# Three-layer decoder block on one core: tokens packed by token-id expert first, and the first two layers, the second norm and the weight splits in one merged pipeline

## The chip, the cores and the metric

The kernel runs on one core of a Trainium2 chip. The metric is the device time of one execution in microseconds, the median of several runs. The core has five engines with an instruction queue each: PE (TensorE, matmuls and transposes), DVE (VectorE), ACT (ScalarE), POOL (GpSimd) and SP (SyncE, which here only issues DMAs). They wait for one another through semaphores; each engine works its own queue in order.

## The reference

2048 tokens of width 512 pass three residual layers. Cut to what matters:

```python
x = x + attn_ref(layernorm(x), w_gate, g_gate, w_down, g_down)   # layer A: gated MLP, ternary weights, 8-bit activations
x = x + xattn_ref(layernorm(x), token_ids, ctx, ctx, ctx)        # layer B: one of 4 experts, chosen by the token's id
x = x + ffn_ref(layernorm(x), gate_w, w_gate, w_up, ...)         # layer C: shared expert and the best 2 of 8 experts

def attn_ref(x, ...):            # A; bitlinear = rmsnorm, rounding to 255 steps per row, weights rounded to -1, 0, 1
    gate, v = split(bitlinear(x, w_gate, g_gate))                # 512 -> 2 * 1408
    return bitlinear(gate * sigmoid(gate) * v, w_down, g_down)   # 1408 -> 512

def xattn_ref(h, token_ids, W, W, W):   # B
    e = min(clip(token_ids, 0, 24999) // 6250, 3)
    return ((silu(h @ W[e].T) * (h @ W[e].T)) @ W[e].T)          # the same 512 x 512 matrix three times

def ffn_ref(h, ...):             # C
    p = softmax(h @ gate_w.T); top 2 of 8
    return sum over the top 2 of p_e * expert_e(h) + shared(h)   # experts 512 -> 352 -> 512, shared 512 -> 704 -> 512
```

## The kernel before

Tokens are worked in tiles of 128 rows, 16 of them (T). Products of B and C are made from 16-bit high and low parts, three matmuls for each (`split_product`: high by high, high by low, low by high). Every layer is a software pipeline: `pipeline(engine, count, stages)` takes a list of (lag, stage) and, in round r, runs each stage on tile r minus its lag, in the order of the list. So the order within a list is the order of an engine's queue within a round, and the lag is how many rounds a stage runs behind. In the middle of a list it makes a hardware loop of two rounds (`Fori`).

- **Routing for B.** At the start DVE and PE compute, from the token ids, where each token goes when tokens are sorted by expert, with each expert padded to whole tiles: 19 tiles (J_B). `invB` lists the tokens of each padded tile, `posB` the place of each token.
- **Layer A** (16 tiles plus fill and drain). SP loads x in token order. DVE: statistics, `swiglu` in four chunks per tile, `g_absmax`, `norm1` (L1052), `d_int` (L1026) and others. POOL: the gains product in two halves (L597), small vectors, `h_lo` (L621). ACT: silu, roundings, evacuations of PSUM. PE: `gate_up` in four chunks of 8 matmuls of 352 columns (L1299), `d_turn` with 11 transposes (L1307), `down` with 11 matmuls of 512 columns (L1316), `x_turn` with 4 transposes. The result x1 is stored, and its norm as high and low halves in `hB_d`. The context matrix is loaded and split during the last rounds (`ctx_chunks`).
- **Layer B** (19 tiles). It starts when all of `hB_d` is stored. POOL gathers the rows of a padded tile, PE transposes them (8 transposes, L1330), ACT evacuates them (L795), then `b_first` (12 matmuls), silu and product, four transposes (L1360), `b_second` (12 matmuls), and a store to `yB_d`. 18 of the 40 chunks of C's expert weights (`wstage`, 544 KB each) are loaded and split beside it, one a round (`split_hi` L789 on ACT, `split_lo` L1102 on DVE).
- **Second norm, stage S** (16 tiles). It starts when all of `yB_d` is stored, and runs in the first 15 rounds of C (S_ROUNDS). SP loads x1, POOL gathers y rows (L630), `residual2` (L1124), statistics, `norm2`, `s_rest`, stores of x2 and `hC_d`, a transpose and the router product (`s_turn`, `s_router`).
- **Layer C.** Rounds 0 to 23 (R0 = 24) work 12 tiles of the shared expert, two halves each; the other 22 weight chunks are split beside them, and after S the top-2 routing is computed on DVE in eight pieces with one C round after each (`beside`). Rounds 24 to 62 are 39 routed tiles (gather, products, store to `yC_d`). The last 8 rounds work the remaining 4 shared tiles, while POOL gathers the two expert rows of every token (L687), DVE sums them (L1246) and SP stores the output in pairs of tiles (`f_store`).

SP's queue has in every round of S, in this order: the next weight chunk (`s_loadw`), `s_stored` (which waits until the stores of x2 and hC of an earlier tile have landed), loads for C, the store of x2, the store of hC, and the load of x1.

## Time and profile before

| | us |
|---|---|
| median of 3 runs | 937.57 (936.64 to 939.38) |
| profiled execution, first to last instruction | 967.5 |
| PE busy | 760.4 (79%) |
| DVE busy | 504.4 (52%) |
| ACT busy | 397.7 (41%) |
| POOL busy | 263.6 (27%) |
| moved by DMA | 127.57 MB, mean 132 GB/s |
| mean granted TensorE clock | 0.912 |

The profiled execution is 29.9 us longer than the median. Its record has a start and a length for each instruction; the times of this document are read on that scale, from the first instruction. PE's busy time is that of matmuls which overlap, so a PE that is 100% busy at full clock sets the pace, and one at 70% may still wait in every round.

### The profile page before, as it was taken

The numbers are of one execution on the slowest core, as the hardware profiler recorded it, in microseconds if no ns is written. First come the engines' busy times: TensorE is split into PE (matmuls) and PEld (weight loads), VectorE is DVE, ScalarE is ACT, GpSimd is POOL, SyncE is SP. The second block draws the span as 40 slices with busy tenths as digits, with TensorE's granted clock in tenths as the row PEclk, the third lists the DMA queues.
The fourth block names the chain that finished last, engine by engine and source line by source line (L and its number), as shares of the span: only waits on it lengthen the run. The fifth ranks groups of instructions, "written<-read, shape, count | busy, mean of one in ns | idle before, by whom it ended". The sixth has DMA issues, their size and how long they took to land.

```text
span 967.5 us, 17562 instructions
## 1 busy us (share of the span) xinstructions
PE 760.4 (79%) x5001; PEld 452.5 (47%) x5017; DVE 504.4 (52%) x861; ACT 397.7 (41%) x567; POOL 263.6 (27%) x401
## 2 busy tenths in 40 slices
PE   0457777777429999749778998899999999999275
PEld 0234443444215555335445655566666666665133
DVE  6779888887714555446564567222222222222146
ACT  5866556656515555335343543122332223231010
POOL 1235665565321111032121000111111111104710
PEclk9979899888559999969898999899999999999679
DMA  9312222212544555267776542122222222226843
GB/s 353 112 34 77 61 70 87 87 66 87 158 159 135 180 179 179 95 209 238 230 215 216 201 148 78 56 88 87 76 77 86 87 78 77 84 77 224 248 138 138
DMA packets 51204, 127.57 MB, mean 132 GB/s; under 512 B 6496, under 2 KB 6496, under 8 KB 50528
## 3 DMA queue, kind: packets, MB, share of 16 engines
q1 hardware_dynamic: 42688, 99.33, 30.5%
q0 software_dynamic: 8480, 27.79, 9.9%
q8 instruction: 19, 0.31, 0.1%
q14 instruction: 17, 0.14, 0.1%
HBM read 87.78 MB, written 39.32 MB: 131 GB/s over the span
## 4 chain that ended last, share of the span: by engine, by line
PE 47%; DMA 10%; issue 4%; another core or an unknown queue 4%; DVE 4%; SPq 2%; ACT 1%; POOL 0%; DVEq 0%; POOLq 0%; ACTq 0%
PE banks L1338 41%; DMA x_d<-w_hi 5%; PE banks L1330 3%; PE banks L1428 2%; DMA x_d<-yrow 2%; DMA hC_d<-w_lo 1%; PE banks L1360 1%; DMA rows<-hC_d 1%; DVE w_hi L1246 0%; DMA rows<-hC_d,idx 0%; SPq L458 0%; SPq L441 0%; DVE w_lo L1102 0%; DMA rows<-hB_d,idx 0%
## 5 line engine op out<-in xcount | busy, mean ns | idle before, releaser
L1338 PE MATMUL banks<-w_hi,hT 128*128 (+1 forms) x1288 | 321.0, 326 | 4.4 <-issue 3.2
L1338 PE MATMUL banks<-w_lo,hT 128*128 (+1 forms) x644 | 209.8, 326 | 0.0
L1338 PEld LDWEIGHTS banks<-w_hi,hT 128*128 128x128 f16 x1288 | 128.0, 99 | 82.2 <-issue 10.6
L1338 PE MATMUL banks<-w_hi,cpT 128*128 (+1 forms) x426 | 142.9, 390 | 10.0 <-issue 8.6
L1299 PE MATMUL banks<-w_hi,w_lo 128*128 128x352 bf16 x384 | 89.3, 350 | 45.6 <-DVE w_hi L1015 34.3
L844 ACT ACTIVATE cs<-banks 128x352 f32<-128x352 f32 x71 | 32.9, 463 | 201.7 <-PE banks L1338 175.5
L1160 DVE TENSOR_TENSOR cs<-banks,cs 128x352 f32<-128x352 f32 x71 | 37.1, 523 | 140.9 <-ACT cs L844 135.0
L1164 DVE TENSOR_TENSOR cpT<-banks,cpT 128x384 f16<-128x384 f32 x71 | 39.5, 556 | 129.3 <-ACT cpT L849 112.6
L1338 PE MATMUL banks<-w_lo,cpT 128*128 (+1 forms) x213 | 83.1, 390 | 5.3 <-issue 5.3
L1330 PE MATMUL banks<-eyeH,rows 128*128 128x128 f16 x584 | 47.6, 225 | 48.2 <-DMA rows<-hC_d 19.6
L1338 PEld LDWEIGHTS banks<-w_lo,hT 128*128 128x128 f16 x644 | 63.9, 99 | 34.5 <-issue 0.8
L849 ACT CAST cpT<-banks 128x384 f16<-128x384 f32 x71 | 33.9, 478 | 96.3 <-PE banks L1428 80.5
L1299 PEld LDWEIGHTS banks<-w_hi,w_lo 128*128 128x128 bf16 x384 | 38.0, 107 | 73.1 <-DVE w_hi L1015 41.5
L628 POOL COPY idx<-invC 128x1 int32 (+1 forms) x39 | 7.1, 182 | 235.6 <-PE banks L1330 163.5
L1338 PEld LDWEIGHTS banks<-w_hi,cpT 128*128 128x128 f16 x426 | 42.3, 99 | 58.7 <-issue 18.6
L1330 PEld LDWEIGHTS banks<-eyeH,rows 128*128 128x128 f16 x584 | 40.0, 101 | 60.6 <-issue 32.5
L839 ACT COPY hT<-banks 128x1024 f16<-128x1024 f16 x55 | 55.6, 1012 | 24.9 <-PE banks L1330 24.9
L597 POOL TENSOR_TENSOR w_hi<-w_hi 128x704 f32<-128x704 f32 x32 | 54.2, 1694 | 32.6 <-DVE w_hi L1015 32.3
L1102 DVE SCALAR_TENSOR_TENSOR w_lo<-wstage,w_hi 128x1088 f32 (+1 forms) x40 | 51.4, 1285 | 4.8 <-ACT w_hi L789 4.8
L1338 PE MATMUL banks<-w_hi 128*128 x152 | 48.3, 379 | 2.3 <-DVE yrow L1116 2.3
L1316 PE MATMUL banks<-w_lo 128*128 128x512 bf16 x161 | 43.9, 427 | 5.0 <-ACT w_lo L751 3.8
L630 POOL DMA_INDIRECT rows<-hC_d,idx x39 | 38.0, 974 | 33.6 <-POOL idx L628 32.4
...
## 6 DMA issues: line engine op xcount, KB each, us to landing
...
yC_d<-yrow SPq DMA_DIRECT2D x39, 256.0 KB, 2.0
w_hi<-x_d SPq DMA_DIRECT2D x20, 256.0 KB
yB_d<-yrow SPq DMA_DIRECT2D x19, 256.0 KB, 2.0
w_hi<-in_wgate SPq DMA_DIRECT2D x3, 1408.0 KB, 9.9
w_hi<-in_x SPq DMA_DIRECT2D x16, 256.0 KB, 2.8
w_lo<-in_x SPq DMA_DIRECT2D x16, 256.0 KB, 3.6
x_d<-w_lo SPq DMA_DIRECT2D x16, 256.0 KB, 2.9
```

The costliest lines, as they stand in the source:

```text
L597: pool.tensor_tensor(swg[s.u][:, at], sw[s.u][:, at], gd[:, at], ALU.mult).then_inc(swg_done, 1)
L630: pool.indirect_dma_start(out=dst[s.u][:] if dst is rows else dst[s.u], out_offset=None, in_=table[:, :], in_offset=bass.IndirectOffsetOnA ...
L839: act.copy(hT[s.u][:].rearrange("p a n -> p (a n)"), bank(0).bitcast(F16)).then_inc(c_ev, 1)
L844: act.activation(cs[:, 0:IC], bank(1 + s.u, IC), ACT.Silu, scale=1.0 / SCALE_C).then_inc(c_sil, 1)
L849: act.copy(cpT[:, 0, :], bank(5, ICP)).then_inc(c_hi_s, 1)
L1102: dve.scalar_tensor_tensor(out=w_lo[:, at], in0=wstage[s.u][:], scalar=SCALE_C, in1=w_hi[:, at], op0=ALU.mult, op1=ALU.subtract).then_inc( ...
L1160: dve.tensor_tensor(cs[:, 0:IC], bank(3 + s.u, IC), cs[:, 0:IC], ALU.mult).then_inc(c_p, 1)
L1164: dve.tensor_tensor(cpT[:, 1, :], bank(5, ICP), cpT[:, 0, :], ALU.subtract).then_inc(c_lo_s, 1)
L1299: mm = pe.matmul(bank(2 * half + c % 2, CW), xqT[s.u][:, k * P:(k + 1) * P], wgT[k][:, at:at + CW], start=(k == 0), stop=(k == KD - 1))
L1316: mm = pe.matmul(bank(7), qdT[s.u][:, k * P:(k + 1) * P], wdT[:, k * D:(k + 1) * D], start=(k == 0), stop=(k == KI - 1))
L1330: mm = pe.transpose(bank(0).bitcast(F16)[:, k * P:(k + 1) * P], source[:, k * P:(k + 1) * P], eyeH[:])
L1338: mm = pe.matmul(to, a(k, pa), w(k, pw), start=(begins and k == 0 and n == 0), stop=(ends and k == steps - 1 and n == 2))
```

## The change

Where each token goes is still computed first, but without padding: `packing` gives `invT`, the tokens in order of their expert, 16 full tiles. From there on all stages work in packed order:

- POOL gathers the rows of x for A twice with that list (`gather_x` for the statistics, `gather_res` for the residual); SP's `load_x` and `load_res` go.
- A tile of B is a window of 128 consecutive packed rows at a computed row `baseB` (`padded_tiles`); it may reach into a neighbour's rows, which are then written again by the tile that owns them. So `b_gather`, the 8 PE transposes and ACT's evacuation go; one DMA that transposes while it moves (`b_load`, `DMA_TRANSPOSE`) brings the window from `hB_d` into `hT`. It and the store `b_store` read their row from `baseB` into a register of SP first.
- B tile j needs only the A tiles up to j, so B runs in the same rounds as A, `b_first` 5 rounds behind (B_LAG) and `b_second` 6. S runs in the same list too: its first tile in round 16. C's round 0 is round 25 (C0). All lists of these 25 rounds are written out straight, without a hardware loop.
- S needs no gather: y is in order. Its POOL gathers go; SP loads y (L512). Its stages are spread wider: `s_stored` is two rounds behind the store it waits for.
- The context matrix is loaded and split in rounds 1 to 4. Weight chunks: 8 in rounds 17 to 24, then two in each of C rounds 0 to 8, then one each.
- Several stages change places in their lists; `b_rows_out` goes from DVE to ACT. PSUM banks are dealt out anew.
- S ends in C round 9 (S_ROUNDS = 10), and the routing pieces stand beside C rounds 10 to 17.
- The output goes out in packed order, so it is scattered row by row: 16 indirect DMAs on POOL, behind its 32 gathers, each waiting for the sum of its tile.

```diff
+B_LAG = 5
+C0 = T + 3 + B_LAG + 1
+S_LAG = T - C0
-S_ROUNDS = T - 1
+S_ROUNDS = T + S_LAG + 3
...
-        CTX_FROM = T + 3 - CTX_ROUNDS
+        CTX_FROM = 1
...
+        W_ONES, W_TWOS = 8, 9
+        W_FROM = C0 - W_ONES
...
+            def b_load(s):
+                if s.t == 0:
+                    sp.wait_ge(routeB, 2)
+                for u in range(2):
+                    sp.wait_ge(hb_out[u], 16 * ((covered(s.t + 1) + 1 - u) // 2))
...
+                before(sp, b_t, s.t, 2)
+                sp.sem_inc(passed["sp"], 1)
+                at = sp.value_load(baseB[0:1, s.t:s.t + 1], min_val=0, max_val=N)
+                sp.dma_start_transpose(hT[s.u][:], hB_d[bass.ds(at, P), :]).then_inc(b_hT[s.u], 16)
...
-            pipeline(sp, TILES, [(W_LAG - 1, s_loadw, w_rest), (-2, s_stored, whole), (-2, c_rows_in, shared_first),
-                                 (-3, s_storex2, whole), (-3, s_storeh, whole), (-5, s_load, whole), (1, c_store),
-                                 (0, c_sum_in, shared_first)], end=S_ROUNDS)
...
+            twos, ones = w_twos(load_w), w_ones(load_w)
+            w_loads = [(twos[0] - 1, *twos[1:]), (ones[0] - 1, *ones[1:])]
+            s_stages = shifted([(2, s_stored), (0, s_storex2), (1, s_storeh), (-1, s_load)], -S_LAG)
...
-            pipeline(pool, T, [(-2, small_x), (1, small_g), (3, small_b), (0, lambda s: gains(s, 0)),
-                               (0, lambda s: gains(s, 1)), (3, h_lo)])
...
+            def gather_x(s):
+                if s.t == 0:
+                    pool.wait_ge(routeB, 1)
...
+                pool.indirect_dma_start(out=xin[s.u], **packed(x, s)).then_inc(x_in[s.u], 16)
...
+            straight(-4, C0, [(-4, gather_x), (-2, small_x), (3, small_b), (1, small_g), (0, lambda s: gains(s, 0)),
+                              (2, gather_res), (3, h_lo), (0, lambda s: gains(s, 1)), (T, s_rstd)])
...
+            for n in range(T):
+                alone(pool, "pool", f_o, n + 1)
+                pool.indirect_dma_start(out=out[:, :], out_offset=bass.IndirectOffsetOnAxis(ap=invT[:, n:n + 1], axis=0),
+                                        in_=xF[:, n * D:(n + 1) * D], in_offset=None).then_inc(f_out, 16)
...
+            stages = [(3, residual1), (B_LAG + 1, b_rest, all_b), (0, lambda s: swiglu(s, 0)), (3, spread1), (3, moments1),
+                      (1, g_absmax), (B_LAG, b_prod, all_b), (0, lambda s: swiglu(s, 1)), (-3, x_spread), (-3, x_moments),
+                      (1, g_reciprocal), (1, g_factor), (-2, x_reciprocal), (-2, x_factor), (3, norm1), (-1, x_int),
+                      (-3, x_center), (1, d_int), (0, lambda s: swiglu(s, 2)), (-3, x_absmax), ctx_chunks(ctx_rest),
+                      (0, lambda s: swiglu(s, 3))]
...
-            pe.wait_ge(ctx_lo, CTX_CHUNKS)
-            pe.wait_ge(x1_done, T)
-            pipeline(pe, J_B, [(0, b_first), (-1, b_turn), (1, b_second), (0, b_turn_a)])
...
+            stages = [(0, lambda s: gate_up(s, 0)), (B_LAG, b_first, all_b), (0, lambda s: gate_up(s, 1)), (2, d_turn),
+                      (B_LAG + 1, b_second, all_b), (0, lambda s: gate_up(s, 2)), (-1, x_turn), (2, down),
+                      (0, lambda s: gate_up(s, 3)), (B_LAG, b_turn_a, all_b)]
```

PE, a round of layer A. Before, between two chunks of `gate_up` (L1299) stand only the transposes of `d_turn` (L1307) and `down` (L1316):

```order
L1299 MATMUL banks<-w_lo 128x352
L1307 MATMUL banks<-w_lo 128x128 [waits d_ev,d_q]
L1307 MATMUL banks<-w_lo 128x128 x10
L1299 MATMUL banks<-w_hi,w_lo 128x352 [waits sw_done]
L1299 MATMUL banks<-w_hi,w_lo 128x352 x2
L1299 MATMUL banks<-w_lo 128x352
L1299 MATMUL banks<-w_hi,w_lo 128x352 x3
L1299 MATMUL banks<-w_lo 128x352
L1316 MATMUL banks<-w_lo 128x512 [waits x1_done,d_ev]
L1316 MATMUL banks<-w_lo 128x512 x10
```

PE, the same place now, from round 6 on (L1423 is `gate_up`, L1433 `d_turn`, L1490 the load of the expert's number, L1458 B's products):

```order
L1423 MATMUL banks<-w_lo 128x352
L1433 MATMUL banks<-w_hi,w_lo 128x128 [waits d_ev,b_lo,x_ev,d_q]
L1433 MATMUL banks<-w_hi,w_lo 128x128 x10
L1490 TENSOR_LOAD expB [waits b_lo,x1_done]
L1490 ISA x2
L1458 ISA
L1458 MATMUL banks<-w_hi,w_lo 128x512
L1458 REGISTER_ALU
L1458 MATMUL banks<-w_lo 128x512
```

What moved: `b_second`'s 12 matmuls stand between `d_turn` and the third chunk, and in the same way `b_first`'s 12 between the first and the second.

DVE, the end of a round of layer A and the start of the next. Before (`norm1` L1052, `d_int` L1026, `residual1` L1034, `swiglu` L1015, `g_absmax` L1021):

```order
L1052 TENSOR_SCALAR w_lo<-w_lo,mv,rstd 128x512 [waits lo_done,hi_done,rs1]
L1002 TENSOR_SCALAR cg<-cg,smG 128x1 [waits g_rec]
L978 SCALAR_TENSOR_TENSOR w_hi<-w_hi,xmv 128x512 [waits x_mom,x_mag]
L1010 REGISTER_ALU
L1015 SCALAR_TENSOR_TENSOR w_hi<-banks,dqx,w_hi 128x352 [waits sil_done]
L983 TENSOR_REDUCE xmax<-w_hi 128x1 [waits x_cen]
L1026 TENSOR_SCALAR w_lo<-w_hi 128x1408 [waits d_T,d_mag]
```

DVE now (`norm1` L1186, `x_int` L1141, `d_int` L1160, `swiglu` L1149):

```order
L1186 TENSOR_SCALAR w_lo<-w_lo,mv,rstd 128x512 [waits lo_done,hi_done,rs1]
L1141 TENSOR_SCALAR w_lo<-w_hi 128x512 [waits x_T,x_mag]
L1112 SCALAR_TENSOR_TENSOR w_hi<-w_hi,xmv,w_lo 128x512 [waits x_mom,x_q]
L1160 TENSOR_SCALAR w_lo<-w_hi 128x1408 [waits d_T,d_mag]
L1149 SCALAR_TENSOR_TENSOR w_hi<-banks,dqx,w_hi 128x352 [waits sil_done]
L1117 TENSOR_REDUCE xmax<-w_hi 128x1 [waits x_cen]
L1149 SCALAR_TENSOR_TENSOR w_hi<-banks,dqx,w_hi 128x352 [waits sil_done]
```

What moved: `d_int` stood behind the last `swiglu` of a round, whose end also starts POOL's second half of the gains; now it stands before the last two.

SP, one round of C with S beside it, inside the loop. Before (L441 weight chunk, L484 rows for C, L462 x2, L467 hC, L458 load of x1):

```order
L441 DMA wstage<-in_wmoe 128x1088
L484 ISA [waits s_hout0,s_x2out0,c_T]
L484 DMA rows<-hC_d 128x1024
L462 ISA [waits s_x2]
L462 DMA x_d<-w_hi 128x512
L467 ISA [waits s_lo,s_hi]
L467 DMA hC_d<-w_lo 128x1024
L458 ISA [waits s_h,s_x2out1]
L458 DMA w_hi<-x_d 128x512
```

SP now, in C rounds 0 to 8 (L500 weight chunk, L516 x2, L521 hC, L510 load of x1, L512 load of y, L547 rows for C):

```order
L500 DMA wstage<-in_wmoe 128x1088 [waits wlo_done] x2
L516 DMA x_d<-w_hi 128x512 [waits s_hout1,s_x2out1,s_x2]
L521 DMA hC_d<-w_lo 128x1024 [waits s_lo,s_hi]
L510 DMA w_hi<-x_d 128x512 [waits x1_out0,b_out1,s_h,s_x2out0]
L512 DMA w_lo<-yB_d 128x512 [waits s_x2]
L547 DMA rows<-hC_d 128x1024 [waits c_T]
```

What moved: two weight chunks are ahead of the loads of x1 and y; the second waits for the round's last `split_lo` on DVE.

## Rows read from the trace of the kernel before

**Rows 1.** Stretches: length, PE, PEld, DVE, ACT, POOL busy, clock, DMA, GB/s

```profile
57.00:267.00 210.00, 149.23 (x856) 83.11 (x869) 178.01 (x278) 126.34 (x197) 118.72 (x159) 0.84 0.27 85
285.00:404.00 119.00, 115.54 (x664) 61.36 (x664) 58.30 (x74) 56.99 (x74) 19.05 (x33) 0.97 0.47 150
541.00:612.00 71.00, 66.16 (x486) 41.14 (x484) 45.39 (x97) 28.06 (x39) 0.18 (x1) 0.98 0.36 120
```

**Rows 2.** Timeline of a round of layer A: start, us, engine, instruction [idle before]

```profile
140.95 2.18 DVE L1026 TENSOR_SCALAR w_lo<-w_hi 128x1408 bf16<-128x1408 f32 x1
149.94 0.61 PE L1299 MATMUL banks<-w_hi,w_lo 128*128 128x352 bf16 x3
150.54 0.61 PE L1299 MATMUL banks<-w_hi,w_lo 128*128 128x352 bf16 x3
154.06 1.67 POOL L597 TENSOR_TENSOR w_hi<-w_hi 128x704 f32<-128x704 f32 x1 [1.83 <-DVE w_hi L1015]
154.30 2.18 DVE L1026 TENSOR_SCALAR w_lo<-w_hi 128x1408 bf16<-128x1408 f32 x1
```

**Rows 3.** Two lines of DVE alone: min/median/max ns, first and last start

```profile
L1026 DVE TENSOR_SCALAR w_lo<-w_hi x16: 889/2180/2186, 64.4 to 258.2; 128x1408 bf16<-128x1408 f32 x16
L1052 DVE TENSOR_SCALAR w_lo<-w_lo,mv,rstd x16: 546/1882/1893, 84.4 to 270.0; 128x512 f32<-128x512 f32 x16
```

**Rows 4.** Chain of work in a round of layer B: start, us, what

```profile
296.35 0.45 PE banks L1330 x8
296.79 2.59 PE banks L1338 x12
299.38 0.44 PE banks L1360 x4
299.82 2.59 PE banks L1338 x12
```

**Rows 5.** Timeline of the start, DVE and PE

```profile
15.85 0.18 DVE L939 CAST invB<-banks 128x19 int32<-128x19 f32 x1 [0.53 <-PE banks L1268]
20.64 0.69 DVE L983 TENSOR_REDUCE xmax<-w_hi 128x1 f32<-128x512 f32 x1
23.77 0.16 DVE L1073 TENSOR_REDUCE wmean<-banks 128x1 f32<-128x4 f32 x1 [0.33 <-PE banks L1278]
37.43 1.06 PE L1299 MATMUL banks<-w_hi,w_lo 128*128 128x352 bf16 x3 [11.31 <-DVE w_lo L1083]
56.52 1.06 PE L1299 MATMUL banks<-w_hi,w_lo 128*128 128x352 bf16 x3 [8.15 <-DVE w_hi L1015]
```

**Rows 6.** DMA issues by line: KB each, median us from issue to landing

```profile
w_hi<-in_wgate SPq DMA_DIRECT2D x3, 1408.0 KB, 9.9
hB_d<-rows SPq DMA_DIRECT2D x16, 256.0 KB, 2.1
rows<-hC_d SPq DMA_DIRECT2D x15, 256.0 KB, 4.0
rows<-hB_d,idx POOLq DMA_INDIRECT x19, 3.8
```

**Rows 7.** SP's waits in stage S: us in total, times, longest; then residual2

```profile
SPq L458 <- DMA x_d<-w_hi: 38.0, 11, 4.6
L1124 DVE SCALAR_TENSOR_TENSOR w_hi<-w_lo,w_hi x16: 684/684/693, 414.7 to 535.7; 128x512 f32<-128x512 f32 x16
```

**Rows 8.** One issue on SP (timeline), then the page's group of weight splits on DVE

```profile
479.01 0.36 SPq L462 DMA_DIRECT2D x_d<-w_hi  x1
...
L1102 DVE SCALAR_TENSOR_TENSOR w_lo<-wstage,w_hi 128x1088 f32 (+1 forms) x40 | 51.4, 1285 | 4.8 <-ACT w_hi L789 4.8
```

**Rows 9.** Chain of two shared rounds of layer C, late in the program

```profile
872.23 5.52 PE banks L1338 x33
884.04 0.34 PE banks L1428 x3
```

**Rows 10.** The page's DMA queue of SP: packets, MB, share of 16 engines

```profile
q1 hardware_dynamic: 42688, 99.33, 30.5%
```

606 lines of the change are left out of this document (350 added, 256 removed).

## The prediction

> **What bounds the kernel now.** Read the stretches first, then look inside each for the wait that ends last. The kernel has four regimes. In layer A, 57 to 267 us, DVE is busy 178.01 of 210 us and PE's clock is granted at 0.84 only [rows 1]: a round takes 13.35 us, the distance of two `d_int` [rows 2], and DVE sets it. Part of that is not work. `d_int` has a median of 2.18 us and once took 0.89; `norm1` has 1.88 and 0.55 at best [rows 3]. In the timeline `d_int` starts 0.24 us behind a POOL product of 1.67 us and ends some 0.75 us behind its end [rows 2]: the two share something, and DVE loses 1.3 us twice, 2.6 us a round. In layer B, 285 to 404 us, PE is the bound: 115.54 of 119 us busy at clock 0.97 [rows 1], and the chain is PE alone, 0.45 + 2.59 + 0.44 + 2.59 = 6.07 us a tile [rows 4]. In stage S the 16 `residual2` are (535.7 - 414.7)/15 = 8.07 us apart, and SP stood 38.0 us waiting for stores of x2 before it issued the next load [rows 7]: a loop through memory sets the pace. From 541 to 612 us nine shared rounds take 71 us [rows 1], though two such rounds need 884.38 - 872.23 = 12.15 us of PE [rows 9], 6.08 each: 16 us go to the routing computed between them. The 39 routed tiles after 612 us and the last shared ones are not changed.
>
> So until 612 us PE works well in B only. The change lays B, which needs PE, beside A, which needs DVE, and hides the emptying of A, the start of B and the start of S. The sum goes by the time at which the first routed round starts, 612 us before.
>
> **Start.** x is gathered only after the packing is known. The last small step of the old routing ends at 16.03 us, and two tiles' statistics were done at 21.33 [rows 5], 5.3 us later; the weights' mean followed at 23.77. The packing has about as many small steps. A gather lands 3.8 us after issue when the queues are quiet; a weight load in this stretch took 9.9 [rows 6]. Statistics then end at 25 to 31 us instead of 21.3, the mean 1.5 to 7 us late. I take 4, nearer to the gather's own row: the first `gate_up` at 41.4 instead of 37.4. Round 0 keeps its length, 56.52 - 37.43 = 19.1 [rows 5], so round 1 starts at 60.5.
>
> **Rounds 1 to 4** have no B yet but all eight context splits. DVE loses the 2.6 us of contention if the new order holds (`d_int` no longer behind the end of the last `swiglu`) and gains two splits of about 1.29 [rows 8]: still 13.3 a round, 53, to 113.7.
>
> **Rounds 5 to 15, A and B together.** PE at full clock: 32 matmuls of `gate_up` at 0.60 us per four (149.94 to 150.54) [rows 2], 4.8; 11 of `down` at 2.59/12 each, 2.4; 15 transposes at 0.45/8, 0.85; B 2 x 2.59 + 0.44, 5.6 [rows 4]. Sum 13.65 us. B's own turn, 0.45, is gone. DVE: 178.01/210 x 13.35 = 11.3, less 2.6, plus two 128x512 steps of 0.68 [rows 7], 10.1, or 12.7 if the contention stays. ACT: 126.34/210 x 13.35 = 8.0 plus three such steps, 10.0 [rows 1]. PE becomes the bound, its idle DVE and ACT hide their additions. Bounds: 13.65, and 16.3 if the contention's 2.6 us stay and stop PE too. I take 14.7: the register load ahead of each B product was hidden under 2.6 us of queued matmuls before, and now has one chunk of 1.2 us ahead. 11 x 14.7 = 162, to 275.4.
>
> The Trainium skill, VectorE: DVE Perf Modes, section "The three transpose paths", gives 1309 ns for a 128x128 transposed by DMA; eight one after another would be 10.5 us a tile, an estimate from that page, and 19 us would be added below by its price. No trace here shows a DMA that transposes.
>
> **Rounds 16 to 24, the rest of B beside S.** Rounds 16 to 18 still have `d_turn`, `down`: PE 5.6 + 3.0 + 0.45 for S's turn, about 9.1; I take 10, 30 us. Then S's loop: a load lands 4.0 us after issue [rows 6], `residual2` 0.7, statistics 0.9, the halves 0.7, three issues of 0.36 [rows 8], 7.4; PE needs about 7. I take the measured 8.1 of S before. Six rounds are 48.6, to 354.0. The transposing DMA is issued a round ahead, so up to about 8 us are hidden here and 14 before. Its cost is in no row. Below: the plain store of the same 256 KB lands in 2.1 us. Near: the gather of the same rows lands in 3.8 [rows 6]. Above: a packet took 0.305 x 16 x 967.5/42688 = 0.11 engine-us [rows 10]; cut into pieces of 256 B the tile is 1024 packets, 7.1 us on 16 engines; in pieces of 128 B, 14.2. I take anything below 8, which costs nothing.
>
> **C rounds 0 to 9.** Here the change adds a wait. SP may issue the second weight chunk only after the last split of DVE's round, and x2, hC, the loads of x1 and y are queued behind it, and `residual2` of the next round behind those. Five issues of 0.36 [rows 8], 1.8; landing 4.0 [rows 6]; then on DVE 0.7 + 0.9 + 0.7, about 1.0 for C's steps, two splits 2.6 [rows 8]. Sum 11.7 us a round, six times, 70; the last S tiles are done by round 6. Round 0 about 9, rounds 7 and 8 with two chunks 8 each, round 9 8. Sum 103, to 457. Bounds for the six: 8.1, the pace of S before with one chunk, and 14.
>
> **C rounds 10 to 23.** 14 x 6.08 = 85 [rows 9], and of the 16 us of routing I keep 14, since its end is no longer the start of the gathers: 99. The first routed round starts at 556, that is 56 us earlier.
>
> **End.** The last store was plain and is now an indirect DMA behind the sum: between 0 and 3.8 us [rows 6], 1.5 taken. The other scatters hide under the last shared rounds.
>
> Sum: 967.5 - 56 + 1.5 = 913 us for a profiled execution. That of before is 29.9 us longer than the median. I put the difference, not a ratio, on the median: 937.57 - 54.5 = **883 us**.
>
> **Rivals.**
>
> - *The doubled weight chunks cost nothing.* If the loads of x1 and y land sooner than DVE's other work ends, S stays at 8.1: 6 x 3.6 = 22 us less, and with a merged round of 14.0 another 8: 853 to 861. For it: SP's waits for stores, 38.0 us, are gone by the wider lag. Against: 1.1 MB more stand ahead of those loads.
> - *The contention stays, or the transposing DMA is a little too slow.* Merged rounds of 16.3: 11 x 1.6 = 18 us more, 901. POOL has two more issues a round, so this is open. Or a transposed tile of 10 to 12 us: only the eight tiles of rounds 16 to 23 feel it, 8 x (11 - 8.1) = 23 us, 906.
> - *Slower than before.* The place is the load of `hT` in B. With T us a tile, T above 8.1 costs 8 (T - 8.1), and above 14.7 also 11 (T - 14.7); the 54.5 us are gone at T = 14.9. Pieces of 128 B give 14.2, almost that; at 20 us a tile 95 + 58 = 153 us are lost and the kernel takes 1036. Stores of A's results and the weight chunks share SP's queue, so it would hit them as well.
> - *Nothing moves*, because the other engines' queues bind at the same places: against it stands that DVE, ACT and PE all have room for the sum of both layers in a 13.35 us round, as worked out.
>
> **How the numbers follow.** The forecast with 868 to 898 has 0.45. The first rival, down to 845, 0.17; still faster 0.02. The second, 898 to 925, 0.22; more of it, to 934, 0.05. Within 0.3%, which is about what a measurement of this kernel tells from no change, 0.02. Slower 0.07. Faster is 0.91. The range 848 to 922 leaves out some 0.18: the slower case, the upper part of the second rival and a little below.
>
> **What would show it.** Layer A's rounds from 5 on 14 to 15.5 us long, PE over 90% busy at a clock near 1; `d_int` and `norm1` near 0.9 and 0.6 us; the first `gate_up` at 39 to 44 us; `hT` landing in under 8 us, and no wait of `b_first` for it; C rounds 1 to 6 about 12 us apart with DVE waiting for the load of y; the first routed round at about 556 us. Wrong would be made most easily by the transposing DMA, then by waits between the four engines inside a merged round, which add up where each queue is in order.

## The result, and the profile after

The changed kernel takes **966.26 us** (median of 4 runs, 965.62 to 969.98), the kernel before beside it 937.11 (4 runs, 934.96 to 939.38). The ratio is 1.031, 95% interval 1.028 to 1.034: **slower by 3.1%**, where 883 us were forecast. 83 us have to be accounted for.

Busy time by stretch of the changed kernel, cut where the forecast cuts (columns as in [rows 1]): rounds 1 to 4, 5 to 15, 16 to 24, C rounds 0 to 9, C rounds 10 to 23, and from the last matmul to the end.

```profile
68.43:127.20 58.77, 37.07 (x183) 19.19 (x187) 45.17 (x74) 35.24 (x52) 28.80 (x40) 0.73 0.32 99
127.20:287.80 160.60, 150.08 (x921) 85.02 (x931) 117.99 (x214) 106.25 (x170) 99.96 (x134) 0.98 0.34 101
287.80:390.10 102.30, 71.45 (x424) 36.28 (x425) 54.88 (x92) 42.45 (x60) 20.37 (x33) 0.90 0.69 207
390.10:539.40 149.30, 80.51 (x579) 49.26 (x580) 53.82 (x88) 44.65 (x59) 6.44 (x14) 0.72 0.45 147
539.40:636.00 96.60, 90.05 (x611) 55.13 (x610) 57.41 (x111) 42.29 (x56) 2.70 (x6) 0.98 0.38 128
938.00:968.30 30.30, 0.24 (x2) 0.00 (x0) 5.82 (x9) 0.00 (x0) 17.23 (x17) 0.58 0.42 156
```

| | forecast, us | measured, us | difference |
|---|---|---|---|
| first `gate_up` at | 41.4 | 49.1 | +7.7 |
| round 0 | 19.1 | 19.4 | +0.3 |
| rounds 1 to 4 | 53 | 58.8 | +6 |
| rounds 5 to 15 (A and B together) | 162 | 160.6 | -1 |
| rounds 16 to 24 | 78.6 | 102.3 | +24 |
| C rounds 0 to 9 | 103 | 149.3 | +46 |
| C rounds 10 to 23 | 99 | 96.6 | -2 |
| first routed round at | 556 | 636 | +80 |
| last sum to the end | about 5 | 24.3 | +19 |

The forecast has no figure for the last row; it is the 3.3 us of the kernel before without its stall (below) and the 1.5 that the forecast adds.

The merged rounds came out at the forecast length: PE is busy 150.08 of 160.6 us at clock 0.98, against 0.84 for layer A alone in [rows 1]. The largest loss is in C rounds 0 to 9: PE is busy 54% of the time there, at a granted clock of 0.72, with DMA at 0.45 and DVE at 36%. No engine is full there; they wait for one another. The waits of that stretch (waiter <- what it waited for: us in total, times, longest):

```profile
PE banks L1450 <- DMA rows<-hC_d: 68.3, 5, 18.0
DVE w_hi L1211 <- DMA w_lo<-yB_d: 45.8, 6, 8.0
```

L1450 are the transposes of the shared expert's rows (`c_turn`), L1211 is `residual2`. One round on SP's queue, DVE and PE, from the timeline (start, us, engine, line; in brackets the idle time before and its releaser):

```profile
399.39 2.48 DVE L1197 SCALAR_TENSOR_TENSOR w_lo<-wstage,w_hi 128x1088 f16<-128x1088 f32 x2
400.70 1.53 SPq L500 DMA_DIRECT2D wstage<-in_wmoe  x2
402.42 0.35 SPq L516 DMA_DIRECT2D x_d<-w_hi  x1
402.87 0.37 SPq L521 DMA_DIRECT2D hC_d<-w_lo  x1
403.42 0.34 SPq L510 DMA_DIRECT2D w_hi<-x_d  x1
403.81 1.41 SPq L512 DMA_DIRECT2D w_lo<-yB_d  x1
405.26 0.75 SPq L547 DMA_DIRECT2D rows<-hC_d  x1
410.73 0.69 DVE L1211 SCALAR_TENSOR_TENSOR w_hi<-w_lo,w_hi 128x512 f32<-128x512 f32 x1 [7.96 <-DMA w_lo<-yB_d]
411.41 1.01 PE L1450 MATMUL banks<-eyeH,rows 128*128 128x128 f16 x8 [10.64 <-DMA rows<-hC_d]
421.22 1.53 SPq L500 DMA_DIRECT2D wstage<-in_wmoe  x2
```

Read it from the top. The two splits of the last round (L1197) free the two weight buffers; SP, which stood waiting for exactly that, issues two chunks of 544 KB, then two stores, then the loads of x1 and y, then the shared rows. Those land at 410.7 and 411.4, with the chunks under way beside them. Only then can `residual2` and `c_turn` start, and behind them in DVE's queue stand the next two splits, which end the loop at 421.22: 20.5 us for this round. The next took 14.5 (the chunks' next issue is at 435.68), and so they alternate, up to 523.4. The long ones are those that load shared rows (L547 at 405.26, 440.15, 474.17 and 507.00), since one load of rows serves two halves: there PE's part, and behind it the splits, wait for the rows too.

At the other end, GpSimd issues the 32 gathers of `yC_d` and then the 16 scatters of the output; the last sum of DVE is L1369:

```profile
896.74 0.95 POOL L746 DMA_INDIRECT w_lo<-yC_d,posC  x1 [28.93 <-DMA yC_d<-yrow]
937.77 1.27 POOL L746 DMA_INDIRECT w_hi<-yC_d,posC  x1 [0.30 <-DVE w_hi L1369]
939.35 1.01 POOL L752 DMA_INDIRECT out_x<-w_hi,invT  x1 [0.30 <-DVE w_hi L1369]
943.21 0.75 DVE L1369 SCALAR_TENSOR_TENSOR w_hi<-w_hi,wtop 128x512 f32<-128x512 f32 x1
959.13 0.97 POOL L752 DMA_INDIRECT out_x<-w_hi,invT  x1 [0.30 <-issue]
```

The first scatter goes out at 939.35, when all sums but three are done, and the other fifteen at 1.3 us each. No engine but GpSimd works from 944 us on. Its last issue ends at 960.1 and lands 2.7 us after it began; from 963 us to the end at 968.3 no engine works and no DMA moves anything.

### The profile page after: what moved, and what is told of

Read it like the earlier page. It is cut to its first block, busy times and chain, and to the rows that moved or that the text cites. A ratio compares the mean times of both kernels' runs of the same rounds, so it can differ in the third digit from the quotient of the medians.

```text
span 968.3 us, 16660 instructions
## 1 busy us (share of the span) xinstructions
PE 741.1 (77%) x4848; PEld 441.0 (46%) x4865; DVE 471.0 (49%) x848; ACT 396.4 (41%) x570; POOL 272.6 (28%) x380
## 3 DMA queue, kind: packets, MB, share of 16 engines
q0 software_dynamic: 9520, 31.20, 10.4%
## 4 chain that ended last, share of the span: by engine, by line
PE 55%; DVE 12%; issue 11%; DMA 7%; POOL 6%; ACT 4%; SPq 1%; POOLq 1%; DVEq 0%; ACTq 0%
PE banks L1458 41%; PE banks L1443 4%; PE banks L1423 3%; PE banks L1450 3%; DMA rows<-hC_d 3%; PE banks L1550 2%; DVE w_lo L1197 2%; DMA w_lo<-yB_d 2%; ACT w_hi L847 2%; POOL out_x L752 1%; POOL w_hi L697 1%; DMA w_hi<-in_x,invT 1%; DVE w_lo L1141 1%; DVE w_hi L1149 1%; POOL smA L646 1%
## 5 line engine op out<-in xcount | busy, mean ns | idle before, releaser
L1458 PE MATMUL banks<-w_hi,hT 128*128 (+1 forms) x1288 | 318.2, 324 | 10.9 <-issue 4.5
L1458 PE MATMUL banks<-w_lo,hT 128*128 (+1 forms) x644 | 208.5, 324 | 0.0
L1458 PEld LDWEIGHTS banks<-w_hi,hT 128*128 128x128 f16 x1288 | 127.0, 99 | 88.2 <-issue 17.3
L1458 PE MATMUL banks<-w_hi,cpT 128*128 (+1 forms) x426 | 145.2, 396 | 1.3 <-DVE cpT L1288 1.3
L1423 PE MATMUL banks<-w_hi,w_lo 128*128 128x352 bf16 x384 | 81.5, 326 | 19.1 <-DVE w_lo L1265 10.8
L1450 PE MATMUL banks<-eyeH,rows 128*128 128x128 f16 x440 | 35.6, 227 | 68.3 <-DMA rows<-hC_d 68.3
L1458 PE MATMUL banks<-w_lo,cpT 128*128 (+1 forms) x213 | 84.5, 397 | 0.0
L1458 PEld LDWEIGHTS banks<-w_lo,hT 128*128 128x128 f16 x644 | 63.4, 98 | 34.2 <-issue 0.6
L1458 PE MATMUL banks<-w_hi,w_lo 128*128 x152 | 53.3, 414 | 18.1 <-DVE w_lo L1206 9.7
L1458 PEld LDWEIGHTS banks<-w_hi,cpT 128*128 128x128 f16 x426 | 43.0, 101 | 47.9 <-issue 8.4
L1450 PEld LDWEIGHTS banks<-eyeH,rows 128*128 128x128 f16 x440 | 30.4, 102 | 75.3 <-DMA rows<-hC_d 54.1
L1423 PEld LDWEIGHTS banks<-w_hi,w_lo 128*128 128x128 bf16 x384 | 38.3, 102 | 46.7 <-DVE w_lo L1265 11.0
L632 POOL TENSOR_SCALAR var<-mv 128x1 f32<-128x1 f32 x32 | 9.6, 299 | 174.6 <-DVE mv L1223 121.3
L1197 DVE SCALAR_TENSOR_TENSOR w_lo<-wstage,w_hi 128x1088 f16<-128x1088 f32 (+1 forms) x40 | 50.8, 1287 | 15.6 <-ACT w_hi L847 15.6
L1149 DVE SCALAR_TENSOR_TENSOR w_hi<-banks,dqx,w_hi 128x352 f32<-128x352 f32 x64 | 37.0, 578 | 38.1 <-ACT w_hi L785 38.1
```

The lines of the kernel that those rows point to most:

```text
L1149: dve.scalar_tensor_tensor(out=sw[s.u][:, c * CW:(c + 1) * CW], in0=bank(2 + c % 2, CW), scalar=dqx[s.u][:], in1=sil[c % 2], op0=ALU.mult, ...
L1197: dve.scalar_tensor_tensor(out=w_lo[:, at], in0=wstage[s.u][:], scalar=SCALE_C, in1=w_hi[:, at], op0=ALU.mult, op1=ALU.subtract).then_inc( ...
L1423: mm = pe.matmul(bank(2 * half + c % 2, CW), xqT[s.u][:, k * P:(k + 1) * P], wgT[k][:, at:at + CW], start=(k == 0), stop=(k == KD - 1))
L1450: mm = pe.transpose(bank(0).bitcast(F16)[:, k * P:(k + 1) * P], source[:, k * P:(k + 1) * P], eyeH[:])
L1458: mm = pe.matmul(to, a(k, pa), w(k, pw), start=(begins and k == 0 and n == 0), stop=(ends and k == steps - 1 and n == 2))
```

## A stall in the tail that must be kept apart

The profile of the kernel before, 30 us above its median, has a stall between 889 and 928 us: PE is busy 13.5 of these 39 us, DVE 4.5 and ACT 1.5, with PE and DVE waiting mostly on "issue" and ACT 25.9 us on what the profile calls "remote", while GpSimd issues its gathers back to back. By their times the runs of the result have it in neither kernel. In the batches of experiments, each of which timed the kernel before beside the others, it came and went for all kernels of a batch together, though not in the same length for each; the kernel before took 966.78, 967.55, 937.32, 936.56 and 968.86 us in five batches (7 runs each), the last three on the same chip. So below, totals are compared only within a batch, and stretches by their traces. Two more profiles of the kernel before frame it:

> The kernel before, unchanged, profiled once more. Its first profile has a stretch from 889 to 928 us in which PE, ACT and DVE wait on 'issue' while GpSimd issues its 32 gathers of yC_d, and its span (967.5 us) is 30 us above the median of the runs. If the stall belongs to the profiled execution only or comes and goes, this span is about 937 to 940 us, the last hT copies stand 12 us apart to the end, and the last matmul ends near 928 us. If the stall is in every execution, the span is again 965 to 970 us with the same gap, and then the runs without a profile have it too, in part.

Measured 970.78 us, with the stall: the copies of `hT` (L839) for the last tiles stand 46 and 14 us apart instead of 12, and between 898 and 925 us PE issues single transposes and matmuls 0.7 to 2.8 us apart.

```profile
882.55 1.01 ACT L839 COPY hT<-banks 128x1024 f16<-128x1024 f16 x1
928.68 1.01 ACT L839 COPY hT<-banks 128x1024 f16<-128x1024 f16 x1
942.71 1.01 ACT L839 COPY hT<-banks 128x1024 f16<-128x1024 f16 x1
```

> The kernel before, unchanged, one more profile. Without the stall: the last five hT copies 12.15 us apart each, the last sum 47 us behind the third last copy, the end 4 us behind the last sum, a span of about 935 us. With it: a span of 965 to 970 us again.

Measured 936.63 us. This is the kernel before without the stall:

```profile
622.60 0.46 ACT L844 ACTIVATE cs<-banks 128x352 f32<-128x352 f32 x1 [3.25 <-PE banks L1338]
878.92 1.01 ACT L839 COPY hT<-banks 128x1024 f16<-128x1024 f16 x1
891.06 1.01 ACT L839 COPY hT<-banks 128x1024 f16<-128x1024 f16 x1
907.53 1.01 ACT L839 COPY hT<-banks 128x1024 f16<-128x1024 f16 x1 [4.30 <-PE banks L1330]
930.66 0.75 DVE L1246 SCALAR_TENSOR_TENSOR w_hi<-w_hi,wtop 128x512 f32<-128x512 f32 x1
```

The last gap is still 16.5 us, 4 more than the others. Its first routed silu (L844) is at 622.60, that of the changed kernel at 640.38: **17.8 us are lost before the routed rounds**. From there to the end it takes 934.7 - 622.6 = 312.1 us, the changed kernel 968.3 - 640.4 = 327.9: **15.8 us are lost behind them**: 21.0 from the last sum to the end (24.3 against 3.3), less 5.2 up to the last sum, 4.3 of which are that gap. The first of the two numbers is less firm than it looks: the changed kernel's first routed silu comes at 634.05 in its second profile and at 633.26 to 639.43 in the kernels below that differ from it only in the tail.

## The experiments

**The changed kernel in a batch with the stall.**

> The changed kernel, unchanged, timed in turn with the kernel before on one chip. The kernel before has now shown two tails: without a stall (937 us in the runs shown first) and with one (967 us in seven executions beside the last four kernels, in both profiles: 30 us in which every engine but GpSimd waits on 'issue' while GpSimd issues 32 gathers). The changed kernel's profile had no such stall. If the stall belongs to the chip or the moment of loading, the two kernels fall into it together and the difference stays 25 to 35 us (before 937, changed 966; or 967 and 995 to 1000). If it belongs to each kernel by itself, the changed kernel stays at 966 and the kernel before is at either 937 or 967.

Measured 986.06 us against 967.55, ratio 1.017 (1.011 to 1.023). Its trace has the stall as well (48 us between two `hT` copies that stood 12 apart in the profile after). Both kernels fall into it together, but the difference is 18.5 us, below the 25 to 35 of the first theory. The trace shows what fits that: GpSimd goes on issuing during the stall, its last scatter goes out 1 us behind the last sum, and the end comes 10 us behind that sum, not 24. So the scatters cost some 20 us only where nothing else is late. The stages before the tail agree with the profile after within 6.5 us.

**Where the weight chunks stand on SP's queue.** Two kernels, one that puts the loads first (the same way in rounds 16 to 24), one that puts the chunks last:

```diff
-            s_stages = shifted([(2, s_stored), (0, s_storex2), (1, s_storeh), (-1, s_load)], -S_LAG)
-            c_stages = [(-2, c_rows_in, shared_first), (1, c_store), (0, c_sum_in, shared_first)]
+            early = [*shifted([(-1, s_load)], -S_LAG), (-2, c_rows_in, shared_first)]
+            s_stages = shifted([(2, s_stored), (0, s_storex2), (1, s_storeh)], -S_LAG)
+            c_stages = [(1, c_store), (0, c_sum_in, shared_first)]
...
-            pipeline(sp, TILES, [w_loads[0], *s_stages, *c_stages], begin=2, end=W_TWOS - 1)
+            pipeline(sp, TILES, [*early, w_loads[0], *s_stages, *c_stages], begin=2, end=W_TWOS - 1)
```

> The changed kernel; on the SP queue the loads of x1 and yB (second norm) and of the shared expert's rows stand first in their round, ahead of the weight chunks, whose issue waits for the split of the round before. Theory 1 (order of the SP queue): C rounds 0 to 9, 17.2 us each in the changed kernel, fall to 9 to 12 us, the 8 us that DVE waits for yB in each round and the 11 to 18 us that PE waits for the rows go, and the rounds 17 to 24 lose 2 to 3 us each too: 50 to 80 us less, 890 to 915 us. Theory 2 (traffic: 1.1 MB of weight chunks in each of these rounds, so the loads land late wherever they are issued; or DVE's work): rounds stay at 15 to 17 us, 945 to 966 us.

```diff
-            pipeline(sp, TILES, [w_loads[0], *s_stages, *c_stages], begin=2, end=W_TWOS - 1)
+            pipeline(sp, TILES, [*s_stages, *c_stages, w_loads[0]], begin=2, end=W_TWOS - 1)
```

> The changed kernel; in C rounds 0 to 9 the two weight chunks are issued behind the loads and stores of their round, the rest of the order as it is. Theory 1 (a wait for the split stands ahead of the loads): the loads of yB are issued up to 3 us earlier, but still behind two waits (x2 stored, hC rows stored), so a part of the gain: 10 to 50 us less, 915 to 955 us. Theory 2 (traffic or DVE's work): no change, 960 to 970 us.

Measured 937.58 (4 runs) and 938.25 us (one run), in a batch with the stall, where the kernel before took 966.78 (ratio of the first 0.969, 0.965 to 0.973). The 890 to 915 us forecast for the first were reckoned without the stall; the changed kernel with the stall took 986.06 in the batch above, 48 more. The stretch of C rounds 0 to 9 of the first, and its waits:

```profile
390.46:484.60 94.14, 73.25 (x580) 45.84 (x581) 54.18 (x88) 44.93 (x59) 6.70 (x14) 0.90 0.69 219
...
PE banks L1451 <- DMA rows<-hC_d: 19.3, 4, 7.0
```

149.3 us became 94.1; DMA's share rose from 0.45 to 0.69 and the granted clock from 0.72 to 0.90; DVE's wait for y is out of the longest ones, and the loads of x1 and y land in 2.7 and 3.1 us (medians) where they took 5.1 and 5.3. The same bytes and the same instructions, so traffic and work are not the cause: the **order on SP's queue** is, 55 us (49 to 56 when the way from the first C product to the first routed silu is compared over all profiles with the old order). The second kernel shows that the place of the chunks alone does it: its first routed silu is at 585.96 us, that of the first at 586.31. One part of the theory fell: in rounds 16 to 24 the early loads of the first kernel moved nothing (first C product at 390.46 us, 390.10 in the changed kernel; 391.12 in the second kernel, which leaves those rounds as they are).

**Where `down` stands on PE's queue.**

```diff
-                      (B_LAG + 1, b_second, all_b), (0, lambda s: gate_up(s, 2)), (-1, x_turn), (2, down),
+                      (B_LAG + 1, b_second, all_b), (0, lambda s: gate_up(s, 2)), (2, down), (-1, x_turn),
```

The reason to try it is in round 3 of the changed kernel, DVE's `norm1` (L1186) and `x_int` (L1141), then PE's `x_turn` (L1409) and `down` (L1443):

```profile
103.39 1.24 DVE L1186 TENSOR_SCALAR w_lo<-w_lo,mv,rstd 128x512 f32<-128x512 f32 x1
104.55 0.41 DVE L1141 TENSOR_SCALAR w_lo<-w_hi 128x512 bf16<-128x512 f32 x1
105.02 0.61 PE L1409 MATMUL banks<-w_hi,w_lo 128*128 128x128 bf16 x4 [6.28 <-DVE w_lo L1141]
105.84 4.43 PE L1443 MATMUL banks<-w_lo 128*128 128x512 bf16 x10 [0.22 <-issue]
```

> The changed kernel; on TensorE, down (11 matmuls of the tile two behind) stands ahead of x_turn (4 transposes of the next tile) instead of behind it. In rounds 1 to 4 of the changed kernel (16 to 19 us each, forecast 13.3) TensorE waits 5 to 6.3 us for x_int with down queued behind that wait. Theory: down fills the wait and the four rounds lose 3 to 4 us each; rounds 5 to 15 (14.7 us, TensorE full) stay: d_turn of tile 15 comes 10 to 16 us earlier than 304. Rival: x_int moves with TensorE, since the wait is DVE's and GpSimd's chain (gains, gather, three small chains): no change, 303 to 304 us, or later.

Measured 974.07 us (one run), with the stall, 12 below the changed kernel in the same batch. The last `d_turn` is evacuated at 289.08 instead of 304.16 us (301.1 to 306.4 in all profiles with the old order). Half of that is not where it was expected: the evacuations (L814) of rounds 6 and 7, in the middle of the merged rounds,

```profile
143.88 1.33 ACT L814 COPY w_lo<-banks 128x1408 bf16<-128x1408 bf16 x1
157.48 1.33 ACT L814 COPY w_lo<-banks 128x1408 bf16<-128x1408 bf16 x1
```

stand 13.60 us apart, against 14.71 in the changed kernel (151.81 and 166.52): the six merged rounds that had taken 14.7 lost 1.1 us each. In the changed kernel each of the five of them that lie between 166 and 240 us has PE idle before `x_turn`, and here none has:

```profile
185.90 0.40 PE L1409 MATMUL banks<-w_hi,w_lo 128*128 128x128 bf16 x4 [0.93 <-DVE w_lo L1141]
```

13.6 is the sum of PE's instructions that the prediction gives as the lower bound (13.65). The 1.05 us that it added for a register load ahead of B's products were this wait. Behind 240 us the changed kernel's own rounds take 13.6 to 13.9 already.

**The first gathers.** The 2.8 MB of down weights are issued behind them:

```diff
+            sp.wait_ge(x_in[1], 16)
             sp.dma_start(wd32, wdown[:]).then_inc(wd_in, 16)
```

> The changed kernel; the 2.8 MB load of the down weights is issued once the first two gathers of x have landed, instead of ahead of them. In the changed kernel the first gather, issued at 17.0 us, lands at 26.9 (9.9 us, where later gathers take 3.6). Theory: it shares the DMA engines with the weights (22.7 us for those 2.8 MB), so it now lands in 4 to 6 us and the first gate_up starts 4 to 6 us earlier, at 43 to 45 us. Rival: a gather's first issue is slow by itself, or the four gate loads are what it shares with: it still takes 8 to 10 us and gate_up starts at 48 to 50 us; then the late down weights cost up to 5 us in round 0.

Measured 980.46 us (one run), with the stall. The first tile's statistics, in the changed kernel and here, both behind a gather issued at 17.0 us:

```profile
26.92 0.69 DVE L1100 BATCH_NORM_STATS2 xstats<-w_hi 128x6 f32<-128x512 f32 x1 [8.39 <-DMA w_hi<-in_x,invT]
```
```profile
20.60 0.69 DVE L1101 BATCH_NORM_STATS2 xstats<-w_hi 128x6 f32<-128x512 f32 x1 [2.03 <-DMA w_hi<-in_x,invT]
```

The gather takes 3.6 us instead of 9.9: it had shared the DMA engines with the weights. Only 3.0 us reach the first `gate_up` (45.8 against 48.8 in the same batch), less than the 4 to 6 of the theory: PE waits for the last ternary weights (DVE's L1266) there.

**The output's order.** Scatters between the gathers:

```diff
+            OUT_LAG = 4
...
+                if n >= OUT_LAG:
+                    scatter(n - OUT_LAG)
+            for n in range(T - OUT_LAG, T):
+                scatter(n)
```

> The changed kernel; each output scatter is issued four tiles behind its gathers, between them, instead of all 16 behind all 32 gathers. Theory A (GpSimd's issue, 1.25 us a gather and 1.27 us a scatter, is the bound of the end): 48 issues take 60 us from 897 us, all the same, and the last scatter goes out at about 957 instead of 959 us, since the queue is full in both orders: at most 5 us less, 961 to 966 us. Theory B (the scatters wait for the last sums): the end comes 15 to 20 us earlier, about 947 to 951 us.

Measured 977.85 us (971.9 to 981.68; 1.011 of the kernel before, 1.006 to 1.016), outside both forecasts, in a batch with the stall and without the changed kernel, so the total decides nothing; its last gather leaves at 959.52 us instead of 937.77. In `e9_all` below, without the stall, the end comes 72.4 us behind the first gather, 71.6 in the changed kernel. Interleaving gains nothing: GpSimd's queue is full either way. Then the same output by plain stores, which leaves its rows in packed order (part of the computation left out):

```diff
-                pool.indirect_dma_start(out=out[:, :], out_offset=bass.IndirectOffsetOnAxis(ap=invT[:, n:n + 1], axis=0),
-                                        in_=xF[:, n * D:(n + 1) * D], in_offset=None).then_inc(f_out, 16)
...
+                sp.wait_ge(f_o, n + 1)
+                sp.dma_start(tiles(out, n), xF[:, n * D:(n + 1) * D]).then_inc(f_out, 16)
```

> The changed kernel without the reordering of its output: the 16 output tiles are written by plain stores on the SP queue, in packed order, not by 16 indirect scatters on GpSimd behind its 32 gathers (so the rows of the output stand in another order than the reference's). If GpSimd's in-order issue is the price, the time from the last sum (944 us) to the end falls from 24 us to about 4 to 6 us (four stores at 12 us in the kernel before): some 18 to 20 us less where the rest is as in the changed kernel. If the indirect writes themselves are slow whoever issues them, or the end waits for something else, less than 8 us.

Measured 981.0 us (one run), with the stall: 2.5 us from the last sum to the end, where the changed kernel of the same batch needed 10. The stall covers most of the price, so it was measured once more without it, on top of three of the mended orders:

> Three of the mended orders (loads, down, down weights), and the output by 16 plain stores on SP in packed order (so its rows stand in another order than the reference's). The kernel with four of them, whose scatters run between GpSimd's gathers, ends 72.4 us behind its first gather of yC_d. Theory A (16 more issues of 1.27 us on GpSimd are the price): here the end comes 50 to 53 us behind the first gather, 20 us less, about 875 us on a chip without the stall. If the indirect writes cost no more than plain ones: 68 to 72 us.

Measured 868.73 us (one run), in a batch without the stall (kernel before 936.56). GpSimd's first issue and DVE's last sum:

```profile
815.70 0.95 POOL L751 DMA_INDIRECT w_lo<-yC_d,posC  x1 [28.93 <-DMA yC_d<-yrow]
863.15 0.75 DVE L1372 SCALAR_TENSOR_TENSOR w_hi<-w_hi,wtop 128x512 f32<-128x512 f32 x1
```

The end comes 51.1 us behind the first gather, 21.3 less than with scatters between the gathers and 20.5 less than in the changed kernel. That is the price of putting the output back in token order. In the changed kernel 16 us of it are GpSimd's issues behind the last sum (944.0 to 960.1). The rest is what follows the last issue: 8.2 us there, 2.7 of them or less for the landing, while with plain stores the end comes 2.9 us behind the last sum. Why nothing moves in the last 5 us and more of the kernels with scatters is not shown.

**All four orders, and two tiles in flight.** Loads first (in the C rounds), `down` first, down weights later, scatters between:

> Four orders of the changed kernel mended at once: in C rounds 0 to 9 the loads stand ahead of the weight chunks on the SP queue (54 us earlier at the first routed round, measured); down ahead of x_turn on TensorE (15 us, measured); the down weights' load behind the first gathers (3 us, measured); each output scatter four tiles behind its gathers. If the gains add, the first routed hT copy comes at about 559 us (changed kernel 628 to 634) and the whole takes 966 - 72 - 3 = about 891 us without the stall at the end, 905 to 915 with it; against the kernel before 0.94 to 0.95 in either case. If the faster A and B rounds hand their gain to the drain (rounds 17 to 24, bound by a chain across engines), the first routed copy comes at 565 to 575 us.

Measured **895.65 us** against 937.32, ratio 0.958 (0.952 to 0.963): faster than both kernels. The gains add, near enough: the first routed silu is at 563.68 us, 77 earlier than in the first profile of the changed kernel (70 than in its second) where the three parts measured alone make 72, and the merged rounds keep their 13.6 us.

The gathers of `yC_d` held to two tiles at a time, to see whether queued gathers cause the stall:

```diff
-                if turn > 0:
-                    alone(pool, "pool", f_y[slot], turn * 32)
+                if n >= 2:
+                    alone(pool, "pool", f_y[(n - 2) % 4], ((n - 2) // 4 + 1) * 32)
```

> The changed kernel; GpSimd lets two tiles' gathers of yC_d be under way, not four, before it issues the next. Theory S (the stall at the end is the other engines' instruction loading, which waits behind the queued gathers on the DMA engines): with half as many queued the hT copies of the last four tiles come closer together (48 us between the third last and the second last in the stalled profiles, 12 without a stall), by 15 us or more, and the end comes 10 to 30 us earlier than 986. Rival (the stall comes with the chip or from elsewhere, however many gathers are queued): again 45 to 50 us there and 980 to 990 us, or, on a chip without the stall, 966 to 972 us.

> The four mended orders with two tiles' gathers in flight. By theory S 885 to 900 us, 0 to 25 us below the same kernel with four in flight; by the rival the same as that kernel within 5 us.

> The kernel before with two tiles' gathers in flight instead of four. Where the kernel before takes 967 us (with the stall), theory S says 937 to 955 us; the rival says 965 to 970. Where it takes 937 us there is nothing to see.

Measured 972.77 (one run), 900.84 (ratio 0.961, 0.956 to 0.967) and 952.47 us (one run). The batch had no stall, so the theory about it was not put to the test. What they show is the price: with the kernel before the last gather goes out at 940.83 instead of 919.25 us, and it takes 15 us more; 5 more for the mended kernel. The first has no partner in its batch.

**Rounds 16 to 24.** First theory: SP waits for the result of `b_second` of its own round before it can issue the next transposing load. B's store one round later takes that wait away:

```diff
-            stages = [(3, store_x1), (4, b_load, all_b), (B_LAG + 1, b_store, all_b),
+            stages = [(3, store_x1), (4, b_load, all_b), (B_LAG + 2, b_store, all_b),
```

> The changed kernel; SP stores the result of a layer-B tile one round later (7 rounds behind its gate_up, not 6), so that it no longer waits for the b_second of the round in which it stands, and the next transposing load of hT, the loads of the second norm and the weight chunk behind it are issued earlier. Theory (the drain's round is a loop b_second, copy, SP's wait, SP's issues, transposing load 5.3 us, b_first, b_second): rounds 16 to 24, 102 us from 288 to 390 us in the changed kernel, fall to 80 to 92 us, and TensorE no longer waits for hT there. Rival (DVE's chain of products, norm and split binds, 10 to 11 us a round by itself): they stay at 98 to 104 us.

> The four mended orders and B's store a round later. If the gains add, 10 to 20 us below the same kernel without it (895.65 us on a chip where the kernel before took 937.32): 876 to 886 us on a chip without the stall, ratio to the kernel before 0.935 to 0.945. By the rival no change: 893 to 898 us, 0.955 to 0.96.

Measured 972.92 (one run) and 895.56 us (ratio 0.956, 0.950 to 0.962), without the stall: nothing gained, the first C product is at 392.09 us. The theory is refuted, and the chain of waits in that kernel shows what is there in its place, one round of 9.33 us:

```profile
343.07 0.48 PE banks L1450 x8
...
344.48 1.12 ACT w_hi L847
...
345.69 1.15 issue
346.83 0.54 DVE w_hi L1229
347.37 0.61 DVE w_lo L1206
...
348.92 2.76 PE banks L1458 x12
351.68 0.44 PE banks L1480 x4
352.12 0.28 PE banks L1458 x12
352.40 0.48 PE banks L1450 x8
```

PE's turn of the second norm, ACT's copy of it and the weights' high half (L847), DVE's low half ("issue" at 345.69 is the time of L1197), `norm2`, `b_rest` (L1206), and only then `b_second`. The split of the weights, put at the end of ACT's and DVE's rounds, stands ahead of layer B's `b_split` and `b_rest`. The next pair moves both halves into waits of their engines:

```diff
-            drain = [*stages, (T + 1, s_split), (T + 2, s_evac), (W_FROM, split_hi, (0, W_ONES))]
+            drain = [*stages[:8], (W_FROM, split_hi, (0, W_ONES)), *stages[8:], (T + 1, s_split), (T + 2, s_evac)]
...
-            drain = [(T + 1, norm2), *stages, (T, residual2), (T, spread2), (T, moments2), (T + 1, s_rest), (T + 3, keep_logits),
-                     (W_FROM, split_lo, (0, W_ONES))]
+            drain = [(T + 1, norm2), *stages, (T, residual2), (T, spread2), (T, moments2), (W_FROM, split_lo, (0, W_ONES)), (T + 1, s_rest),
+                     (T + 3, keep_logits)]
```

> The changed kernel; in rounds 17 to 24 ACT splits the weights' high half ahead of the copy of b_second's result, where it waits for TensorE, and DVE the low half ahead of the second norm's rest, where it waits for ACT, instead of both at the round's end. Theory (ACT's 1.12 us and DVE's 1.29 us stand in a loop of 9.3 us a round: s_turn, s_evac, split, split, norm2, b_rest, b_second): the rounds lose 1 to 2.4 us each, the first C round's gate_up comes at 372 to 382 us instead of 390. Rival (another loop of nearly the same length stands behind, such as the transposing load or TensorE's own order): less than 5 us earlier.

> The four mended orders and the splits moved as in the other kernel of this pair. If the gains add, 8 to 18 us below the four alone (895.65 us where the kernel before took 937.32): 878 to 888 us, ratio to the kernel before 0.937 to 0.948; by the rival 891 to 896 us, 0.951 to 0.957. On a chip with the stall at the end both kernels are 15 to 30 us longer.

Measured 982.42 (one run) and 899.2 us, with the stall (in the second only in part: its last `hT` copies stand 19 and 24 us apart instead of 12); the kernel before took 968.86, the ratio of the second is 0.926 (0.920 to 0.933). That ratio looks better than the one of `e9_all`, but only because the kernel before has the whole stall in it. The first C product is at 384.44 us, 5.7 earlier than in the first profile of the changed kernel, but only 1.8 earlier than in its second (386.29). On top of the four orders it is at 365.86, and the kernel with plain stores, whose splits stand as before, has it at 365.45 (first routed silu at 558.73 and 559.22). So no gain is shown: the rival, another loop of nearly the same length, was right.

What sets the profiles apart goes with the clock. From the last evacuation of `d_turn` to the first C product the changed kernel took 86.1 us at a granted clock of 0.88 and 82.1 at 0.92, `e13_bstore_later` 89.1 at 0.83, the kernel with plain stores 80.5 at 0.94; the two with moved splits took 81.8 and 82.0, both at 0.92. PE's busy time differs by as much as the length does: 58.1 and 53.6 us in the two profiles of the changed kernel. Two neighbouring rounds of `e13_bstore_later`, the second the one above (length, busy times, then granted clock, DMA share and GB/s):

```profile
332.05:343.07 11.02, 8.40 (x51) 4.06 (x50) 5.28 (x9) 3.99 (x7) 0.79 (x2) 0.85 0.70 198
343.07:352.40 9.33, 6.70 (x51) 3.62 (x50) 5.19 (x9) 4.19 (x7) 0.78 (x2) 1.00 0.70 201
```

The same 51 matmuls take 1.7 us more of PE's time in the first, and since `b_second` is part of the loop (4.45 us there, 2.76 in the second), the round is 1.7 us longer. PE is idle 2.6 us in either.

## Why the prediction was wrong, step by step

- **Start, +7.7 us.** The forecast took the landing "nearer to the gather's own row" (3.8 us) and not that of a load among the weights (9.9) [rows 6]. It was 9.9 to the tenth, and `e8_wdown_later`, with 3.6 us, shows that the down weights were the reason. Of the 7.7 us 3.0 came back with it; in both kernels PE then waits for the last ternary weights, and what makes those late was not tested. The row of a transfer in the same stretch was the better one.
- **Rounds 1 to 4, +6 us.** The term was DVE's work. What the trace has instead is PE idle for 20.3 us before `x_turn`, with `down` queued behind that wait; `e6_down_first` gave back some 8 us of it. That GpSimd's small steps ahead of `x_int` set the rest is read from the trace and not tested. `d_int` did fall to 0.89 us, as forecast; `norm1` did not (median 1.24 us), so part of the contention stayed.
- **Rounds 5 to 15, right** in their length, in part by luck: PE's 13.65 are exact, the 1.05 us on top were `down` behind `x_turn`, not the register load, and happened to have its size.
- **The transposing load, right.** The 19 loads of `hT` land in 3.2 to 5.3 us, and PE waited 3.8 us for them in all:

```profile
DMA to landing us min/median/max: 3.2/3.8/5.3
```

The plain load of the same size (`rows<-hC_d`) has a median of 3.9. So the rival that ends slower, by this load, is refuted, though its sign came true by other mechanisms. The Trainium skill's 1309 ns for a 128x128 transposed by DMA (VectorE: DVE Perf Modes, "The three transpose paths") would be 10.5 us for these eight, by the estimate of the prediction; the trace gives 3.8. The Trainium skill, Advanced Engine Details and Errata, section "X-Bar Transpose (TRN2)", says that transposing DMAs are as fast as regular ones, and this trace agrees. (By the prediction's own formula the gain is gone at 14.8 us a tile, not 14.9; nothing hangs on it.)
- **Rounds 16 to 24, +24 us.** The step that failed is "I take the measured 8.1 of S before". A pace measured for one pipeline alone, which went through SP's loads, was used for two that share PE's, ACT's and DVE's queues. Their round is the chain shown for `e13_bstore_later`: 9.33 us at the full clock, 11.0 where the granted clock is 0.85; the last rounds of the changed kernel have a mean of 10.4 (five distances of `residual2`, 329.6 to 381.8). So of the 24 us some 7 are that longer loop and some 7 the clock, which the forecast had at full speed there; the other 9 or so are open, and neither moving B's store nor moving the splits gained anything.
- **C rounds 0 to 9, +46 us.** The mechanism was named ahead (the second chunk's wait on SP, with everything queued behind it) and is shown by `e2_loads_first` and `e3_weights_last`. The step that failed is "Sum 11.7 us a round, six times, 70", by its size: the rounds took 14.2 to 20.5, 17.5 in the mean, on to round 8. Two things were left out that the traces show: the loads of x1 and y land in 5.1 and 5.3 us (medians) with two chunks just ahead of them, not in 4.0 (2.7 and 3.1 with the loads first); and the shared expert's rows stand in the same queue behind them, so that PE is on the loop and every second round takes some 5.5 us more. A third is read from the trace only: ACT's half of the splits stands behind PE's turn. The wait was priced as one loop through DVE, and it was one through four queues, SP, DVE, PE and ACT. The upper bound of 14 was a guess with no row behind it. With the loads first the stretch takes 94.1 us, less than the 103 of the forecast.
- **C rounds 10 to 23, right** (96.6 for 99).
- **The reference point.** 612 us was taken for the start of the routed rounds before. Round 23's silu is at 612.71 and the first routed one at 625.83 in that profile, while the 636 us measured after is a mark 4.4 us ahead of the first routed silu. By that mark it was 621.4 before, so all that follows was priced some 10 us too long.
- **End, +19 us.** "The other scatters hide under the last shared rounds" is the step that failed. The rule of the whole prediction, that each queue is in order, was not put to GpSimd: 32 gathers of 1.25 us fill 40 of the 41 us that the last shared rounds give, and the 16 scatters come behind them. One row of the trace before, the distance of two gathers, would have shown it: 16 more of them are 20 us. What was priced was a scatter's landing (2.7 us measured); most of what the scatters cost is their issue, 16 us, and some 5 us at the very end stay unexplained.

Together: 80 us before the first routed round, less 10 for the mark, plus 19 at the end, less the 5 by which the way to the last sum was shorter than before, is some 85 us: the profile's span of 968.3 us less 883. The median is 2 us below that span, which gives the 83.
